# Expert blocks of two halves of 64 slots, side by side in TensorE's column tiles

## The chip, the cores and the metric

The kernel runs on 1 core of one Trainium2 chip. Times are microseconds (us) of device time of one execution; a kernel's time is the median of its runs.

## What is computed

One layer on `x` of shape (2, 1024, 256): a spiking recurrence, a gated mixture of convolutions and a delta-rule attention, a second recurrence, and a mixture of eight experts. Only the last part is touched:

```python
xf = x.reshape(-1, d)                      # 2048 tokens of 256
logits = xf @ gate_w.T + gate_b
top1 = jnp.argmax(logits, axis=-1)         # one expert per token
for e in range(8):
    h = jax.nn.relu(xf @ w1[e].T + b1[e])  # 256 -> 1024
    y = h @ w2[e].T + b2[e]                # 1024 -> 256
    out = out + jnp.where((top1 == e)[:, None], y, 0)
```

Its result is added to the residual stream. Everything is fp32.

## The kernel before

The stages run one after the other, each a function with its own block of per-engine programs: `load_and_spike`, `project`, `fir`, `attend`, `mix`, `recur`, `experts`. They are joined by semaphores written out by hand, and each engine does its instructions in the order of its program. `project` and `fir` matter here only as places where TensorE already works in column tiles: at L372 four matmuls with 32 columns of weights write partitions 0, 32, 64 and 96 of one bank, and at L574 sixteen to thirty-two such matmuls follow each other, four by four. A matmul in fp32 leaves two records in the trace, each with its own load of weights.

`experts` sorts the 2,048 tokens by expert, so that each token is computed by its own expert alone. First the routing: VectorE finds each token's expert (`hot`), TensorE counts them (L1881, L1882), VectorE works out how many blocks of 128 slots each expert needs (`more`, `nblk`, `first`, L1994 to L1999), each token's slot (`place`, `slot`), and from that the lists `slot_token` (which token sits in a slot) and `eid_i` (which expert a block belongs to). An expert's tokens fill whole blocks, the last one in part, so up to 16 + 7 = 23 blocks (`BLOCKS`) are always computed; empty slots hold an index out of range and are skipped by the transfers. Meanwhile TensorE turns the state `h` into rows (`turn`, L1874), ScalarE copies them and writes them to memory (`h_rows`, L1952, L1954), and the weights `w2` of six experts are still being loaded (L1829); `w1`, all of it, and `w2` of two experts are there already.

Then the blocks, g = 0 to 22:

- GpSimd fetches the block's rows of `h` (`fetch_x`, L1843) and of the residual (`fetch_z`, L1851) by indirect transfers into two buffers each, and at the end scatters the result `y` to `out` (L1862). Its order is: fetch x of g+3, wait for y of g, scatter it, fetch z of g+2.
- TensorE: `turn_in` (L1902) turns the rows, two matmuls of 128 columns; `hidden` (L1911) multiplies them by `w1` of the block's expert, 2 halves n x 2 parts c, 512 columns each; `turn_hidden` (L1929) turns the 1,024 hidden values in eight matmuls; `output` (L1920) multiplies by `w2`, 8 parts k, 256 columns each. The order is: `hidden(g)`, `turn_in(g+1)`, `output(g-1)`, `turn_hidden(g)`. The expert's number is read into a register (L1933), and the weights are addressed with it.
- VectorE copies `hid` out of its banks (L2059), copies the turned input (`xt`, L2052), and adds the residual (L2067) and the bias `b2` (L2069) to the result. Its order is: `hid_out(g)`, `x_out(g+1)`, `y_out(g-1)`.
- ScalarE adds `b1` and applies the relu, on the way from the turned bank to `ht` (L1962), eight operations a block.

Of the kernel before, what the change touches and what calls it, by code (L numbers as in the profile page):

```python
# [19 lines left out]
P = 128  # L20
# [18 lines left out]
BLOCKS = B * T // P + E - 1  # L39
# [1429 lines left out]
def expert_constants(sb):  # L1469
# [7 lines left out]
    g.edges = sb("moe_edges", [P, TILES])  # L1477
    g.ids = sb("moe_ids", [P, BLOCKS])
# [283 lines left out]
def experts(nc, d, m, out):  # L1762
# [5 lines left out]

    TOK = B * T
    TILES = TOK // P  # L1770
    K2 = EH // P
    with ExitStack() as own:
# [14 lines left out]
        more = sb("more", [P, E, TILES])  # L1787
# [10 lines left out]
        upto = sb("upto", [P, BLOCKS, E])  # L1798
        eid = sb("eid", [P, BLOCKS])
        eid_i = own.enter_context(nc.sbuf_tensor("eid_i", [1, BLOCKS], I32))  # L1800
        row = free_zw.rearrange("p (a n) -> p a n", n=D)
        xin = [sb(f"xin{i}", [P, D]) for i in range(2)]
# [11 lines left out]
                 "ht_psum", "ht_ready", "y_psum", "y_half", "y_ready")  # L1814
# [5 lines left out]
        out_rows = out.rearrange("b t d -> (b t) d")  # L1820
        block = own.enter_context(nc.Block())
# [47 lines left out]
        def _(pe):  # L1869
# [62 lines left out]
            def expert(g):  # L1932
                return pe.value_load(eid_i[0:1, g:g + 1], min_val=0, max_val=E - 1)  # L1933
# [15 lines left out]
        def _(act):  # L1949
# [6 lines left out]
            for g in range(BLOCKS):  # L1956
                e = act.value_load(eid_i[0:1, g:g + 1], min_val=0, max_val=E - 1)
                if g:
                    act.wait_ge(s.y_psum, g)
                for k in range(K2):  # L1960
                    act.wait_ge(s.ht_psum, g * 2 + (k // (K2 // 2) + 1))
                    nc.scalar.activation(ht[:, k, :], tr_bank[k // (K2 // 2)][:, k % (K2 // 2) * P:(k % (K2 // 2) + 1) * P],  # L1962
                                         ACT.Relu, bias=b1[:, bass.ds(e, 1), k]).then_inc(s.ht_ready, 1)

        @block.vector
        def _(dve):
# [27 lines left out]
            nc.vector.tensor_tensor(more[:], cum[:, :, TILES].unsqueeze(2).broadcast_to([P, E, TILES]),  # L1994
                                    edges[:].unsqueeze(1).broadcast_to([P, E, TILES]), ALU.is_gt).then_inc(s.r, 1)
# [7 lines left out]
            nc.vector.scalar_tensor_tensor(place[:], wide(first), float(P), by_tile, ALU.mult,  # L2003
# [22 lines left out]
            for part in (slice(0, TILES // 2), slice(TILES // 2, TILES)):  # L2026
# [4 lines left out]
            nc.vector.tensor_tensor(upto[:], first[:].unsqueeze(1).broadcast_to([P, BLOCKS, E]),  # L2031
                                    ids[:].unsqueeze(2).broadcast_to([P, BLOCKS, E]), ALU.is_le).then_inc(s.r, 1)
# [14 lines left out]

            def x_out(g):
# [12 lines left out]
            def y_out(g):  # L2061
                e = dve.value_load(eid_i[0:1, g:g + 1], min_val=0, max_val=E - 1)
# [161 lines left out]
```

## Time and profile before

| | |
|---|---|
| median of 3 runs | 989.38 us (986.22 to 990.27) |
| the profiled execution, its own time | 986.34 us |
| its span | 984.4 us |
| busy: TensorE, its weight loads, VectorE, ScalarE, GpSimd | 74%, 46%, 67%, 52%, 26% |
| mean granted clock of TensorE | 0.871 |
| start of the stage `experts`, of its first `hidden`, end of the span | 756.5, 785.9, 984.4 us |

The busy shares are means over stages with different limits; what a change of one stage is worth is read in that stage. A record of TensorE lasts from its start to its modelled end, and consecutive ones overlap, so the distance between two starts is the cost of one, not its length. Where the chain of waits names an instruction, the length is its share of the chain. Instructions are named by line of the kernel before.

### The profile page before, as it was taken

Reading aid. Unit: us, or ns where it says so; the run is one execution under the profiler, and the core shown is the slowest. Engines: PE = TensorE matmul, PEld = TensorE weight load, DVE = VectorE, ACT = ScalarE, POOL = GpSimd, SP = SyncE. Lnnn points to the kernel's source line nnn. Section 1 sums busy time; section 2 is a strip of 40 time slices with the busy share of each in tenths; the row PEclk is TensorE's granted clock in tenths of the full one; section 3 lists DMA queues with packets and bytes.
Section 4 is the critical chain, followed back from the end, with each engine's and each line's share of the span. In section 5 each row is a group of like instructions: output and inputs, shape, how many; then the busy total and the mean of one; then the engine's idle time right before and its main releaser. Section 6 shows DMA issues by size and latency. Waiting matters only on the chain. (4 is left out here: it accounts for less than half of the span.)

```text
span 984.4 us, 15091 instructions
## 1 busy us (share of the span) xinstructions
PE 724.7 (74%) x5694; PEld 451.0 (46%) x5694; DVE 656.4 (67%) x929; ACT 514.6 (52%) x842; POOL 257.6 (26%) x231
## 2 busy tenths in 40 slices
PE   2840009787766187783986878999997599999995
PEld 1310004333555186772443443444446466777763
DVE  4999986967745987357698744999997233333331
ACT  5878764753333353555562348999993122222221
POOL 0000000001102000000332403988994223433331
PEclk9985558988999678997987889999996599999998
DMA  5640000001891000003000017600002811111100
GB/s 200 219 134 0 0 0 22 1 0 43 229 252 35 1 3 24 3 3 99 1 0 1 22 65 267 233 1 1 0 1 60 299 32 39 45 43 37 38 12 0
DMA packets 35881, 60.68 MB, mean 62 GB/s; under 512 B 8187, under 2 KB 22523, under 8 KB 35426
## 3 DMA queue, kind: packets, MB, share of 16 engines
q1 hardware_dynamic: 30194, 51.31, 16.6%
q0 software_dynamic: 3312, 6.31, 2.1%
q10 hardware_dynamic: 2304, 2.10, 0.6%
q8 instruction: 47, 0.77, 0.3%
q14 instruction: 24, 0.20, 0.1%
HBM read 55.23 MB, written 7.21 MB: 63 GB/s over the span
## 5 line engine op out<-in xcount | busy, mean ns | idle before, releaser
L1962 ACT ACTIVATE xT<-x_tr,moe_b 128x128 f32<-128x128 f32 x184 | 50.1, 383 | 145.5 <-PE x_tr L1929 145.5
L1911 PE MATMUL x_hid<-w,moe_xt 128*128 x184 | 84.6, 603 | 0.9 <-DVE moe_xt L2052 0.7
L1920 PE MATMUL x_y<-w,xT 128*128 x368 | 83.3, 379 | 2.1 <-ACT xT L1962 2.1
L1159 POOL TENSOR_TENSOR path<-path,mix_pr 128x1280 f32<-128x1280 f32 x16 | 38.7, 2448 | 144.8 <-DVE mix_pr L1393 144.8
L2059 DVE COPY xT<-x_hid 128x512 f32<-128x512 f32 x46 | 31.9, 692 | 63.5 <-PE x_hid L1911 63.5
L1920 PEld LDWEIGHTS x_y<-w,xT 128*128 128x128 f32 x368 | 68.2, 190 | 11.1 <-issue 2.8
L1713 DVE TENSOR_TENSOR_SCAN w<-r_bank,w 128x512 f32<-128x512 f32 x56 | 69.7, 1246 | 0.2 <-ACT r_bank L1647 0.2
L217 PE MATMUL bad_sum<-spike_bad,ones 128*128 128x16 f32 x2 | 0.6, 384 | 84.1 <-ACT spike_outside L183 84.1
L1587 PE MATMUL r_bank<-recur_h_other,w1h 128*128 128x512 f32 x128 | 60.3, 593 | 0.7 <-ACT recur_h_other L1627 0.7
L1583 PE MATMUL r_bank<-hs,eye 128*128 128x512 f32 x112 | 57.2, 592 | 1.8 <-DVE h L1694 1.8
L213 PE MATMUL w_bank<-spike_wbuf,spike_pick 128*128 128x512 f32 x80 | 39.6, 650 | 23.3 <-DMA spike_wbuf<-in_gW 23.3
L475 DVE SCALAR_TENSOR_TENSOR proj_y<-proj_pre,mix_st,proj_y 128x1024 f32<-128x1024 f32 x36 | 46.2, 1284 | 10.9 <-ACT proj_y L438 9.8
L2067 DVE TENSOR_TENSOR moe_y<-x_y,moe_zin 128x256 f32<-128x256 f32 x23 | 9.7, 423 | 64.1 <-PE x_y L1920 64.1
L1862 POOL DMA_INDIRECT out<-moe_y,slot_token x23 | 23.6, 1026 | 107.4 <-DVE moe_y L2069 107.4
L1911 PEld LDWEIGHTS x_hid<-w,moe_xt 128*128 128x128 f32 x184 | 33.8, 194 | 35.6 <-issue 35.6
L1673 POOL TENSOR_TENSOR w<-w,recur_h_other 128x512 f32<-128x512 f32 x32 | 37.8, 1182 | 45.8 <-ACT w L1637 45.2
L390 PE MATMUL pj<-hs,mix_st 128*128 128x512 f32 x96 | 45.8, 624 | 2.3 <-PEq L65 2.3
L1587 PE MATMUL r_bank<-h,w1h 128*128 128x512 f32 x96 | 45.1, 592 | 0.0
L1701 DVE TENSOR_TENSOR r_bank<-r_bank,xT 128x512 f32<-128x512 f32 x56 | 38.1, 680 | 8.1 <-ACT r_bank L1633 8.1
L1647 ACT ACTIVATE r_bank<-r_bank,recur_leak,recur_leak_neg 128x512 f32<-128x512 f32 x56 | 42.1, 751 | 1.9
L649 DVE COPY path<-fir_z_bank 64x256 f32<-64x256 f32 x64 | 27.0, 422 | 21.6 <-PE fir_z_bank L584 20.0
L161 ACT ACTIVATE spike_count<-spike_line,spike_mid 128x2048 int16<-128x2048 f32 x8 | 39.1, 4887 | 1.1 <-DVE spike_line L244 1.1
(286 smaller groups left out, 1769.2 us busy)
## 6 DMA issues: line engine op xcount, KB each, us to landing
spike_wbuf<-in_gW SPq DMA_DIRECT2D x8, 1280.0 KB, 6.3
w<-in_w1T SPq DMA_DIRECT2D x8, 1024.0 KB, 12.1
w<-in_w2T SPq DMA_DIRECT2D x8, 1024.0 KB, 14.5
fir_band<-in_band_l SPq DMA_DIRECT2D x11, 512.0 KB
fir_band<-in_band_m SPq DMA_DIRECT2D x11, 312.0 KB
mix_st<-in_band_l SPq DMA_DIRECT2D x5, 512.0 KB
xT<-in_xT SPq DMA_DIRECT2D x4, 512.0 KB, 6.7
xT<-in_xT SPq DMA_DIRECT2D x2, 1024.0 KB, 6.1
```

What stands on the lines that cost most here:

```text
L161: nc.scalar.activation(count[i][:, 2:].rearrange("p (t s) -> p s t", s=SUB), line[u % 2][:], ACT.Relu, bias=mid[:]).then_inc(rounded, 1)
L213: last = nc.tensor.matmul(w_bank[:], pick[:, at:at + P], wbuf[:, ch % 2, i, :], start=(ch == 0 and i == 0), stop=(ch == CHUNKS - 1 and i = ...
L390: last = nc.tensor.matmul(pj[u % 2][:, n * N:(n + 1) * N], w[:, i, k, c * P:(c + 1) * P], m.hs[:, k * B + b, n * N:(n + 1) * N], start=(k ...
L475: nc.vector.scalar_tensor_tensor(out, pre[:, u % 2, k:k + T], wc[:, i, c, k:k + 1], out, ALU.mult, ALU.add).then_inc(conv_step if k < KQ - ...
L1159: nc.gpsimd.tensor_tensor(x, x, w, ALU.mult).then_inc(s.weighted, 1)
L1583: nc.tensor.matmul(out, m.eye[:], zw[:, c * B + b, t0:t0 + N], start=True, stop=False)
L1587: last = nc.tensor.matmul(out, wg[:, k, c * P:(c + 1) * P], state[u // UNITS % 2][:, k * B + b, t0:t0 + N], start=False, stop=(k == C - 1))
L1647: nc.scalar.activation(out, out, ACT.Identity, bias=leak[:, c:c + 1], scale=leak_neg[:, c:c + 1]).then_inc(s.j_ready, 1)
L1713: nc.vector.tensor_tensor_scan(change[:, r, :], j_bank[u % RING][:], rest[:, r, :], first, ALU.mult, ALU.add).then_inc(s.change_ready, 1)
L1911: last = nc.tensor.matmul(hid_bank[n][:], xt[:, c, :], m.w1[:, bass.ds(e, 1), c, n * N:(n + 1) * N].rearrange("p o n -> p (o n)"), start=( ...
L1920: last = nc.tensor.matmul(y_bank[:], ht[:, k, :], w2[:, bass.ds(e, 1), k, :].rearrange("p o n -> p (o n)"), start=(k == 0), stop=(k == K2 ...
L1962: nc.scalar.activation(ht[:, k, :], tr_bank[k // (K2 // 2)][:, k % (K2 // 2) * P:(k % (K2 // 2) + 1) * P], ACT.Relu, bias=b1[:, bass.ds(e, ...
```

## The change

A block of 128 slots becomes two halves of 64, and each half has its own expert. The slots of an expert are padded to whole halves, so 32 + 7 halves at most, in (32 + 8) / 2 = 20 blocks. `eid_i` has an entry for each half. Where one matmul took 128 columns of weights (the tokens) and multiplied them by one expert's matrix, there are now two with 64 columns each, into partitions 0 to 63 and 64 to 127 of the same bank (`side(0)`, `side(1)`). The first reads its expert's matrix in place, addressed by a register; the second reads a copy with a fixed address: `w1_copy`, made by GpSimd (`copy_w1`), and `w2_copy`, made by VectorE (`copy_w2`), two buffers each, in room that the states `h` and `hs` leave free. TensorE waits for `w1_copied` before `hidden` and for `w2_copied` before `output`, which now waits for its activations in two parts. ScalarE makes 16 operations of 64 columns for 8 of 128, and VectorE adds `b2` half by half. The turns stay as they were.

```diff
-BLOCKS = B * T // P + E - 1
+HALF = P // 2
+BLOCKS = (B * T // HALF + E) // 2
...
+        w2_copy = free_zw[:, 0:2 * K2 * D].rearrange("p (i k n) -> p i k n", i=2, k=K2)
+        w1_copy = m.h[:].rearrange("p j t -> p (j t)")[:, 0:2 * C * EH].rearrange("p (i c n) -> p i c n", i=2, c=C)
...
+            def copy_w1(g):
+                if g >= BLOCKS:
+                    return
+                if g >= 2:
+                    pool.wait_ge(s.hid_psum, 2 * (g - 1))
+                e = pool.value_load(eid_i[0:1, 2 * g + 1:2 * g + 2], min_val=0, max_val=E - 1)
+                nc.gpsimd.tensor_copy(w1_copy[:, g % 2], m.w1[:, bass.ds(e, 1)].rearrange("p o c n -> p (o c) n")).then_inc(s.w1_copied, 1)
+
+            pool.wait_ge(s.turned, TILES)
+            pool.wait_ge(s.eid_ready, 1)
+            copy_w1(0)
...
             fetch_x(2)
+            copy_w1(1)
             for g in range(BLOCKS):
                 fetch_x(g + 3)
-                pool.wait_ge(s.y_ready, g + 1)
+                copy_w1(g + 2)
+                pool.wait_ge(s.y_ready, 2 * (g + 1))
...
             def hidden(g, e):
                 pe.wait_ge(s.xt_ready, g + 1)
+                pe.wait_ge(s.w1_copied, g + 1)
                 for n in range(EH // N):
+                    cols = slice(n * N, (n + 1) * N)
                     if g:
                         pe.wait_ge(s.hid_ready, 2 * (g - 1) + n + 1)
                     for c in range(C):
-                        last = nc.tensor.matmul(hid_bank[n][:], xt[:, c, :], m.w1[:, bass.ds(e, 1), c, n * N:(n + 1) * N].rearrange("p o n -> p (o n)"),
-                                                start=(c == 0), stop=(c == C - 1))
+                        nc.tensor.matmul(hid_bank[n][side(0), :], xt[:, c, side(0)],
+                                         m.w1[:, bass.ds(e, 1), c, cols].rearrange("p o n -> p (o n)"),
+                                         start=(c == 0), stop=(c == C - 1), skip_group_check=True)
+                        last = nc.tensor.matmul(hid_bank[n][side(1), :], xt[:, c, side(1)], w1_copy[:, g % 2, c, cols],
+                                                start=(c == 0), stop=(c == C - 1), skip_group_check=True)
                     last.then_inc(s.hid_psum, 1)
 
             def output(g, e):
-                pe.wait_ge(s.ht_ready, g * K2 + K2)
+                pe.wait_ge(s.w2_copied, g + 1)
                 if g:
                     pe.wait_ge(s.y_half, g)
                 for k in range(K2):
-                    last = nc.tensor.matmul(y_bank[:], ht[:, k, :],
-                                            w2[:, bass.ds(e, 1), k, :].rearrange("p o n -> p (o n)"), start=(k == 0), stop=(k == K2 - 1))
+                    if k % (K2 // 2) == 0:
+                        pe.wait_ge(s.ht_ready, 2 * (g * K2 + k + K2 // 2))
+                    nc.tensor.matmul(y_bank[side(0), :], ht[:, k, side(0)],
+                                     w2[:, bass.ds(e, 1), k, :].rearrange("p o n -> p (o n)"),
+                                     start=(k == 0), stop=(k == K2 - 1), skip_group_check=True)
+                    last = nc.tensor.matmul(y_bank[side(1), :], ht[:, k, side(1)], w2_copy[:, g % 2, k, :],
+                                            start=(k == 0), stop=(k == K2 - 1), skip_group_check=True)
                 last.then_inc(s.y_psum, 1)
...
                 for k in range(K2):
                     act.wait_ge(s.ht_psum, g * 2 + (k // (K2 // 2) + 1))
-                    nc.scalar.activation(ht[:, k, :], tr_bank[k // (K2 // 2)][:, k % (K2 // 2) * P:(k % (K2 // 2) + 1) * P],
-                                         ACT.Relu, bias=b1[:, bass.ds(e, 1), k]).then_inc(s.ht_ready, 1)
+                    turned = tr_bank[k // (K2 // 2)][:, k % (K2 // 2) * P:(k % (K2 // 2) + 1) * P]
+                    for x in range(2):
+                        nc.scalar.activation(ht[:, k, side(x)], turned[:, side(x)], ACT.Relu,
+                                             bias=b1[:, bass.ds(e[x], 1), k]).then_inc(s.ht_ready, 1)
...
+            def copy_w2(g):
+                if g >= BLOCKS:
+                    return
+                if g >= 2:
+                    dve.wait_ge(s.y_psum, g - 1)
+                e = dve.value_load(eid_i[0:1, 2 * g + 1:2 * g + 2], min_val=0, max_val=E - 1)
+                nc.vector.tensor_copy(w2_copy[:, g % 2], w2[:, bass.ds(e, 1)].rearrange("p o k n -> p (o k) n")).then_inc(s.w2_copied, 1)
...
                 dve.wait_ge(s.y_half, g + 1)
-                nc.vector.tensor_tensor(y[g % 2][:], y[g % 2][:], b2[:, bass.ds(e, 1), :].rearrange("p o n -> p (o n)"),
-                                        ALU.add).then_inc(s.y_ready, 1)
-
+                for x in range(2):
+                    nc.vector.tensor_tensor(y[g % 2][side(x)], y[g % 2][side(x)],
+                                            b2[side(x), bass.ds(e[x], 1), :].rearrange("p o n -> p (o n)"),
+                                            ALU.add).then_inc(s.y_ready, 1)
+
+            dve.wait_ge(s.w2_in, 16 * (E - W2_AHEAD))
+            dve.wait_ge(s.rows_out, 16 * TILES)
+            copy_w2(0)
             x_out(0)
+            copy_w2(1)
             for g in range(BLOCKS):
                 hid_out(g)
                 if g + 1 < BLOCKS:
                     x_out(g + 1)
                 if g:
                     y_out(g - 1)
+                    copy_w2(g + 1)
             y_out(BLOCKS - 1)
```

How the orders stand, on two engines. `ISA` is the reading of an address register, `TENSOR_LOAD` the load of the expert's number. TensorE, one `hidden` of a block, before (`w` is `w1`):

```order
L1911 ISA
L1911 MATMUL x_hid<-w,moe_xt 128x512
L1911 ISA
L1911 MATMUL x_hid<-w,moe_xt 128x512
L1911 ISA
L1911 MATMUL x_hid<-w,moe_xt 128x512
L1911 ISA
L1911 MATMUL x_hid<-w,moe_xt 128x512
L1902 MATMUL x_x<-eye,moe_xin 128x128 x2
```

and in the changed kernel (`h` is the room of the copy of `w1`), its first three pairs:

```order
L1934 ISA
L1934 MATMUL x_hid<-w,moe_xt 64x512
L1937 MATMUL x_hid<-h,moe_xt 64x512
L1934 ISA
L1934 MATMUL x_hid<-w,moe_xt 64x512
L1937 MATMUL x_hid<-h,moe_xt 64x512
L1934 ISA
L1934 MATMUL x_hid<-w,moe_xt 64x512
L1937 MATMUL x_hid<-h,moe_xt 64x512
```

Each matmul has become two of half the height, of which only the first needs a register. GpSimd, one turn of its loop, before:

```order
L1862 DMA out<-moe_y,slot_token 2048x256
L1851 DMA moe_zin<-z_rows,slot_token 128x256
L1843 DMA moe_xin<-h_rows,slot_token 128x256
L1862 DMA out<-moe_y,slot_token 2048x256
```

and in the changed kernel:

```order
L1883 DMA out<-moe_y,slot_token 2048x256
L1870 DMA moe_zin<-z_rows,slot_token 128x256
L1862 DMA moe_xin<-h_rows,slot_token 128x256
L1846 TENSOR_LOAD eid_i
L1846 ISA x2
L1847 ISA
L1847 COPY h<-w 128x2048
L1883 DMA out<-moe_y,slot_token 2048x256
```

A copy of 128 x 2048 elements now stands between the fetch of x and the wait for the next result.

## Rows read from the trace of the kernel before

**Rows 1.** Page: head, and the granted clock in 40 slices, in tenths.
```profile
span 984.4 us, 15091 instructions
...
PEclk9985558988999678997987889999996599999998
```

**Rows 2.** Chain that ended last, experts: start us, us, what (a steady block).
```profile
873.00 3.44 PE x_hid L1911 x8
876.44 0.22 PE x_x L1902 x2
876.66 3.46 PE x_y L1920 x16
880.11 0.87 PE x_tr L1929 x8
```

**Rows 3.** Instructions by line and form: xcount | busy us, mean ns | idle, releaser.
```profile
L1911 PE MATMUL x_hid<-w,moe_xt 128*128 x184 | 84.6, 603 | 0.9 <-DVE moe_xt L2052 0.7 <-issue 0.2
L1920 PE MATMUL x_y<-w,xT 128*128 x368 | 83.3, 379 | 2.1 <-ACT xT L1962 2.1
```

**Rows 4.** Timeline, TensorE, stages with column tiles: start us, us, engine, line.
```profile
169.49 0.16 PEld L372 LDWEIGHTS ps<-proj_sq,mix_st 128*32 128x32 f32 x8
169.49 1.07 PE L372 MATMUL ps<-proj_sq,mix_st 128*32 128x512 f32 x8
170.49 3.70 PE L390 MATMUL pj<-hs,mix_st 128*128 128x512 f32 x8
...
208.28 3.60 PE L390 MATMUL pj<-hs,mix_st 128*128 128x512 f32 x8
211.81 1.07 PE L372 MATMUL ps<-proj_sq,mix_st 128*32 128x512 f32 x8
...
252.20 2.18 PE L574 MATMUL fir_y_bank<-fir_band,fir_vt 128*32 128x128 f32 x64 [0.68 <-ACT fir_vt L611]
254.55 0.66 PE L584 MATMUL fir_z_bank<-eye,w1h 128*128 128x128 f32 x4 [0.17 <-ACT w1h L623]
```

**Rows 5.** Timeline, one steady block, VectorE, ScalarE, GpSimd and the transposes.
```profile
871.97 1.04 PE L1929 MATMUL x_tr<-eye,xT 128*128 128x128 f32 x8
...
872.74 0.43 DVE L2069 TENSOR_TENSOR moe_y<-moe_y,b 128x256 f32<-128x256 f32 x1
872.76 2.18 ACT L1962 ACTIVATE xT<-x_tr,moe_b 128x128 f32<-128x128 f32 x8 [5.81 <-PE x_tr L1929]
873.99 1.03 POOL L1862 DMA_INDIRECT out<-moe_y,slot_token  x1 [4.31 <-DVE moe_y L2069]
...
874.76 0.69 DVE L2059 COPY xT<-x_hid 128x512 f32<-128x512 f32 x1 [1.59 <-PE x_hid L1911]
875.33 1.04 POOL L1851 DMA_INDIRECT moe_zin<-z_rows,slot_token  x1 [0.30 <-issue]
...
876.67 1.00 POOL L1843 DMA_INDIRECT moe_xin<-h_rows,slot_token  x1 [0.31 <-issue]
```

**Rows 6.** Instructions by line and form, whole span: the nearest rows for the copies.
```profile
L549 POOL COPY path<-fir_vt 128x2048 f32<-128x2048 f32 x2 | 4.0, 2024 | 14.3 <-DVE xT L640 14.3
L1673 POOL TENSOR_TENSOR w<-w,recur_h_other 128x512 f32<-128x512 f32 x32 | 37.8, 1182 | 45.8 <-ACT w L1637 45.2
L468 DVE TENSOR_SCALAR proj_y<-proj_pre,mix_st 128x1024 f32<-128x1024 f32 x8 | 5.9, 736 | 8.8 <-ACT proj_pre L434 8.8
L235 DVE TENSOR_SCALAR w1h<-xT 128x512 f32<-128x512 f32 x8 | 3.4, 423 | 4.1 <-DMA xT<-in_xT 4.1
L1424 DVE TENSOR_TENSOR mix_o<-mix_o,mix_rs 128x1024 f32<-128x1024 f32 x3 | 3.7, 1225 | 0.1
```

**Rows 7.** Windows before the first block: us, busy by engine, PEclk, DMA share, GB/s.
```profile
780.00:782.00 2.00, 0.00 (x0) 0.00 (x0) 0.00 (x0) 0.00 (x0) 0.62 (x1) 0.50 0.74 247
782.00:783.00 1.00, 0.00 (x0) 0.00 (x0) 0.00 (x0) 0.00 (x0) 0.69 (x2) 0.50 0.00 1
```

More of the change, by code:

```diff
@@ L1476, in expert_constants @@
     g.before = sb("moe_before", [P, P])
-    g.edges = sb("moe_edges", [P, TILES])
-    g.ids = sb("moe_ids", [P, BLOCKS])
+    g.edges = sb("moe_edges", [P, B * T // HALF])
+    g.ids = sb("moe_ids", [P, 2 * BLOCKS])
     g.starts = sb("moe_starts", [P, BLOCKS + 1])
@@ L1786, in experts @@
         same = sb("same", [P, E, 1 + TILES])
-        more = sb("more", [P, E, TILES])
+        more = free_z[:, TILES * P:TILES * P + E * TOK // HALF].rearrange("p (e n) -> p e n", e=E)
         nblk = sb("nblk", [P, 1 + E])
@@ L1797, in experts @@
         slot_token = own.enter_context(nc.sbuf_tensor("slot_token", [P, BLOCKS], I32))
-        upto = sb("upto", [P, BLOCKS, E])
-        eid = sb("eid", [P, BLOCKS])
-        eid_i = own.enter_context(nc.sbuf_tensor("eid_i", [1, BLOCKS], I32))
+        upto = free_z[:, TILES * P + E * TOK // HALF:][:, 0:2 * BLOCKS * E].rearrange("p (g e) -> p g e", e=E)
+        eid = sb("eid", [P, 2 * BLOCKS])
+        eid_i = own.enter_context(nc.sbuf_tensor("eid_i", [1, 2 * BLOCKS], I32))
         row = free_zw.rearrange("p (a n) -> p a n", n=D)
+        w2_copy = free_zw[:, 0:2 * K2 * D].rearrange("p (i k n) -> p i k n", i=2, k=K2)
+        w1_copy = m.h[:].rearrange("p j t -> p (j t)")[:, 0:2 * C * EH].rearrange("p (i c n) -> p i c n", i=2, c=C)
         xin = [sb(f"xin{i}", [P, D]) for i in range(2)]
@@ L1813, in experts @@
                  "tokens_ready", "eid_ready", "turned", "row_ready", "picked", "x_psum", "xt_ready", "hid_psum", "hid_ready",
-                 "ht_psum", "ht_ready", "y_psum", "y_half", "y_ready")
+                 "ht_psum", "ht_ready", "y_psum", "y_half", "y_ready",
+                 "w1_copied", "w2_copied")
         s = namedtuple("ExpertSemaphores", names)(*(sem(n) for n in names))
@@ L1820, in experts @@
         out_rows = out.rearrange("b t d -> (b t) d")
+        side = lambda x: slice(x * HALF, (x + 1) * HALF)
         block = own.enter_context(nc.Block())
@@ L1956, in _ @@
             for g in range(BLOCKS):
-                e = act.value_load(eid_i[0:1, g:g + 1], min_val=0, max_val=E - 1)
+                e = [act.value_load(eid_i[0:1, 2 * g + x:2 * g + x + 1], min_val=0, max_val=E - 1) for x in range(2)]
                 if g:
@@ L1993, in _ @@
             dve.wait_ge(s.r, n)
-            nc.vector.tensor_tensor(more[:], cum[:, :, TILES].unsqueeze(2).broadcast_to([P, E, TILES]),
-                                    edges[:].unsqueeze(1).broadcast_to([P, E, TILES]), ALU.is_gt).then_inc(s.r, 1)
+            nc.vector.tensor_tensor(more[:], cum[:, :, TILES].unsqueeze(2).broadcast_to([P, E, TOK // HALF]),
+                                    edges[:].unsqueeze(1).broadcast_to([P, E, TOK // HALF]), ALU.is_gt).then_inc(s.r, 1)
             dve.wait_ge(s.r, n + 1)
@@ L2001, in _ @@
             dve.wait_ge(s.r, n)
-            nc.vector.scalar_tensor_tensor(place[:], wide(first), float(P), by_tile, ALU.mult,
+            nc.vector.scalar_tensor_tensor(place[:], wide(first), float(HALF), by_tile, ALU.mult,
                                            ALU.add).then_inc(s.r, 1)
@@ L2029, in _ @@
                                         ALU.is_equal).then_inc(s.slots_ready, 1)
-            nc.vector.tensor_tensor(upto[:], first[:].unsqueeze(1).broadcast_to([P, BLOCKS, E]),
-                                    ids[:].unsqueeze(2).broadcast_to([P, BLOCKS, E]), ALU.is_le).then_inc(s.r, 1)
+            nc.vector.tensor_tensor(upto[:], first[:].unsqueeze(1).broadcast_to([P, 2 * BLOCKS, E]),
+                                    ids[:].unsqueeze(2).broadcast_to([P, 2 * BLOCKS, E]), ALU.is_le).then_inc(s.r, 1)
             dve.wait_ge(s.r, n + 10)
@@ L2061, in y_out @@
             def y_out(g):
-                e = dve.value_load(eid_i[0:1, g:g + 1], min_val=0, max_val=E - 1)
+                e = [dve.value_load(eid_i[0:1, 2 * g + x:2 * g + x + 1], min_val=0, max_val=E - 1) for x in range(2)]
                 dve.wait_ge(s.y_psum, g + 1)
```

6 lines of the change are left out of this document (3 added, 3 removed).

## Prediction

> **What bounds the kernel now.** The change touches the last stage alone, the experts, so I first asked where that stage lies and whether TensorE's clock is whole there. The 40 slices show a granted clock of 9 tenths or more in the seven slices before the last, which are the blocks from 787 to 960 us; it is low in the two slices before them, and 8 in the last [rows 1]. The chain of waits then says what a block consists of: matmuls of TensorE end to end, 3.44 us `hidden`, 0.22 the turn of the next input, 3.46 `output`, 0.87 the turns of `hid`, so 7.98 us from one `hidden` to the next, with no wait between them [rows 2]. The groups by line agree: over all 23 blocks, TensorE idled 0.9 us before `hidden` and 2.1 before `output` [rows 3]. The timeline shows the others: in one block GpSimd has three transfers to issue (1.03, 1.04 and 1.00), VectorE four short operations and ScalarE eight activations in 2.18 us [rows 5]. So TensorE bounds every block, a record of 512 columns costs 3.44/8 = 0.43 us, one of 256 costs 3.46/16 = 0.216, one of 128 costs 0.87/8 = 0.109.
>
> **What is removed.** Blocks go from 23 to 20 (16 + 7 against (32 + 8)/2); the number is fixed by the code. If a block kept its 7.98 us, this is 3 x 7.98 = 23.9 us less. Everything below is what is paid back.
>
> **The matmuls themselves.** Each matmul of `hidden` and `output` becomes two with 64 columns of weights, so 24 records a block become 48. If the two of a pair run at the same time, a block still needs 7.98. The nearest rows are two stages of this kernel with tiles of 32 columns. At L372 eight records of 512 columns, four tiles, take 1.00 us to the start of the next group, not 8 x 0.43 = 3.44; at L574 64 records of 128 columns end after 2.18, so 16 rounds of four take (2.18 - 0.27)/16 = 0.119 each, near 0.109 [rows 4] (0.27 is what a record lasts beyond its place in the stream: 1.04 for eight against 7 x 0.109 [rows 5]). So tiles do run side by side, and the loss is between 0 and 0.01 us a round. A block has 24 rounds: 0 to 0.24 us. I take 0, because the L574 rounds have four loads of weights in 0.109 us, and `output` has two in 0.216.
>
> **Going in and out of column tiles.** The turns stay 128 wide, so each block goes into column tiles twice and comes out twice. One such excursion is priced from the stage at L372 and its neighbours [rows 4]. In: the eight records at 208.28 would release the next at 208.28 + 3.44 = 211.72, and L372 begins at 211.81: 0.09. Inside: 1.00 for two rounds of 0.43: 0.14. Out: the group behind it takes 3.70 where an undisturbed one takes 3.60: 0.10. Together 0.33 us. Low end 0.29: where turns follow, four of them take 0.66 (L584) against 1.04 - 4 x 0.109 = 0.60, so 0.06 in place of 0.10. High end 0.36: the eight loads of 32 columns at L372 are over in 0.16 us, and 64 columns may show some 0.03 more. I take 0.33, since `hidden` and `output` are streams of the same length as those at L390 and L372. There are 39 excursions (20 `hidden`, 20 `output`, of which the last `hidden` runs straight into `output` 18): 39 x 0.33 = 12.9 us. A block costs 7.98 + 0.66 = 8.64.
>
> **The copy of w1, on GpSimd.** 2,048 elements a partition: L549 did that in 2.02 us [rows 6]. It lies after the three transfers of its turn, and `hidden` waits for it. From the start T of the turns (871.97): the second add of y begins at T + 0.77 and ends at T + 1.20; the added half is another 0.43, with a gap 0.5; GpSimd begins 0.82 later (873.99 against 873.17 [rows 5]), so at T + 2.5, its transfers follow at steps of 1.34, and the copy runs from T + 6.5 to T + 8.5. It is for the `hidden` two blocks on, which begins at T + 0.87 + 3.44 + 0.22 + 3.46 + 0.87 + 3 x 0.33 = T + 9.85. So it is hidden, with 1.3 us to spare. The load of the expert's number on GpSimd has no row; 0 to 0.6 us (two of the gaps of 0.30 between its transfers) still fits.
>
> **The copy of w2, on VectorE.** L235 and L468 took 423 ns for 512 and 736 for 1,024 elements, so 2,048 cost 0.74 + 2 x 0.31 = 1.36 us; at the rate of an operation with two inputs, 1.23 for 1,024 (L1424), about 2.3 [rows 6]. It stands behind the adds of y, so T + 1.7 to T + 3.1 (4.0). Queued behind it are the copies of `hid`, the first of which could begin at T + 3.1; 0.9 late costs nothing, because the turns that need it start after T + 8. Cost 0; if it were not covered, 20 x 1.36.
>
> **ScalarE.** Sixteen activations of 64 columns in place of eight of 128: at most 16 x 0.27 = 4.4 us [rows 5], T + 0.8 to T + 5.2. `output` starts at about T + 5.2 and now asks for the first eight only. Cost 0 in a block.
>
> **Ends.** In the last block nothing covers: the second half add 0.5, and `output`'s second half may wait up to 8 x 0.27 - 8 x 0.216 = 0.4 for activations [rows 5]; 0.7 us together. At the start `copy_w2(0)` needs the last weights; the share of the transfer engines falls from 0.74 to 0.00 at 782 us [rows 7], so it ends at about 783.4, before x is there; while it runs, GpSimd prepares the fetch of x. 0 to 1.4, I take 0.3. Routing: 128 elements more in two operations, 48 fewer in four, at 1 ns each ((0.69 - 0.43)/256 [rows 5]): 0.1. `copy_w1(0)` and `copy_w1(1)` run while GpSimd or TensorE waits for rows anyway: 0.
>
> **Sum.** -23.9 + 12.9 + 0.7 + 0.3 + 0.1 = -9.9 us against the profiled execution, which took 986.34 us (span 984.4): 976.4. The median of the runs shown lies 3.0 higher, 989.38, and on it the forecast is **979.4 us**.
>
> **Rivals.**
> (B) GpSimd becomes the bound, *slower*. The place is TensorE's wait for the copied w1 before `hidden`. GpSimd's turn may grow by 1.3 us free of charge; of each us beyond, half falls on every block, since the chain from one y to the fetch, the copy and the y two blocks later spans two blocks. The gain of 9.9 is gone when it has grown by 1.3 + 2 x 9.9/18 = 2.4 us. For it: no row shows this copy beside VectorE's; at the rate of GpSimd's two-input operation (1,182 ns for 512 [rows 6]) the copy takes 4.7, 2.7 more, and if GpSimd also stands still for VectorE's 1.36 it is 4.1 more: a block of 10.0, 1004 us. Against: L549 ran at 1 ns per element. 1004 us, chance 0.08. The Trainium skill ("SBUF — State Buffer", section "SBUF: two separate sides") has VectorE's copy of fp32 lock GpSimd out of preparing transfers; by it only the part from T + 2.5 to T + 3.1 counts, and no run here shows it yet.
> (C) The weight loads come out into the open. Each of 24 rounds would show a load; all eight loads at L372 are over in 0.16 us, so at most that, and I take 0.1: 24 x 0.1 x 20 = 48 us, 1027 us. Against: at L372 the loads of both rounds are recorded within the first 0.16 us, so before the first round has streamed [rows 4]. Chance 0.04. The Trainium skill ("TensorE: Matmul & The Clock Gate", Part 3, "The mechanism") says that a load overlaps running matmuls only if the row groups differ, which column tiles do not; by that rule this case holds. The rows speak against it.
> (D) The pairs do not overlap at all: 20 x 6.90 more, 1117 us; chance 0.02, against L372 and L574 both [rows 4].
> (E) Excursions are dearer, no change. If each way shows the whole tail of a record (0.16: 3.60 less 3.44) and a load of 0.1 to 0.2, an excursion is 0.6, 39 cost 23.4: 990 us. Half way there, 984 to 990. Chance 0.11.
>
> **Chances and range.** The forecast case has 0.75. Its own range is 972 to 985: excursions at 0.29 (-1.6), an execution like the profiled one rather than the median (-3), rounds at +0.24 a block (+4.8), a fetch held back (+1). To hold 8 in 10 it reaches into E: 971 to 989. What a measurement of this kernel tells from no change is about 0.5%, 4.9 us. Faster by more than that: 0.75; within it: 0.11 (E); slower: 0.14 (B, C and D).
>
> **What would show it.** `hidden` to `hidden` at 8.64 us; pairs of records starting within a few hundredths; eight `hidden` rounds still 3.44 apart from their borders; gaps of about 0.1 at each of four borders; TensorE idle before `hidden` near zero with GpSimd's copy ending over 1 us ahead; GpSimd's COPY at 2.0 and VectorE's at 1.4; granted clock 1.00 from 800 us on. It is wrong if TensorE's waits name GpSimd's copy (B), if records of a pair start 0.2 to 0.4 us apart (C, D), or if the borders are 0.2 or more (E).

## The result, and the profile after

The changed kernel takes 975.69 us (median of 4 runs, 973.89 to 978.99), the kernel before beside it 989.83 (986.22 to 990.97): a ratio of 0.9857 with a 95% interval of 0.9833 to 0.988, 14.1 us less. The forecast was 979.4, range 971 to 989, faster at 0.75.

The profiled execution of the changed kernel was its slowest, 978.99 us. Page, head and granted clock (compare [rows 1]):

```profile
span 977.2 us, 16350 instructions
...
PEclk9985558988898758898879879999998579999998
```

Spans differ by 7.2 us only, medians by 14.1. SyncE's rows show why: the stage `experts` begins with the first load of `w2`, and that came at 756.48 before and at 762.74 after, 6.3 us later, behind stages that the change does not touch.

Timeline of SyncE, kernel before, then changed kernel (start us, us, line, x count):

```profile
756.48 15.71 SPq L1826 DMA_DIRECT2D w<-in_w2T  x6
```
```profile
762.74 17.15 SPq L1833 DMA_DIRECT2D w<-in_w2T  x6
```

So I measure the stage from that load to the end of the span: 227.9 us before, 214.5 after, -13.4, close to the medians. In full_width, whose stages ahead are those of the changed kernel, it came at 758.58: the delay belongs to the execution. Over all profiled executions of this study that load came anywhere from 756.5 to 762.7. A steady block, from the chain (against [rows 2]; `L1934` and `L1937` are the two matmuls of `hidden`, `L1948` and `L1951` those of `output`, `L1960` the turns):

```profile
866.99 1.02 PE x_tr L1960 x8
868.01 0.57 PE x_hid L1934
...
871.60 0.37 PE x_x L1923 x2
871.97 0.36 PE x_y L1948
...
875.57 1.02 PE x_tr L1960 x8
876.60 0.57 PE x_hid L1934
```

`hidden` to `hidden` is 8.58 us where it was 7.98. Each part that begins behind a change of width is longer in its first piece: 0.57 for 0.43, 0.37 for 0.22, 0.36 for 0.216, 1.02 for 0.87. That is 0.15 at each of four borders (a border is the place where a matmul 128 columns wide stands next to one of 64), 0.60 a block. The timeline of TensorE at two of them:

```profile
866.61 0.38 PE L1948 MATMUL x_y<-w,xT 128*64 x1
...
866.92 0.86 PEld L1960 LDWEIGHTS x_tr<-eye,xT 128*128 128x128 f32 x8 [0.38 <-issue]
866.92 1.09 PE L1960 MATMUL x_tr<-eye,xT 128*128 128x128 f32 x8
867.95 0.64 PE L1934 MATMUL x_hid<-w,moe_xt 128*64 x1
...
868.42 0.59 PE L1934 MATMUL x_hid<-w,moe_xt 128*64 x1
868.43 0.59 PE L1937 MATMUL x_hid<-h,moe_xt 128*64 128x512 f32 x1
```

The last round of `output` would have been over at 866.61 + 0.216 = 866.83; the turns begin 0.09 later. The eight turns would have ended at 866.92 + 0.87 = 867.79 and take 0.05 longer (1.09 for 1.04), and `hidden` begins at 867.95, 0.1 behind them. The two of a pair start within 0.01 us, and rounds still cost 0.43 and 0.216. The loads of weights show one thing more. In the kernel before, the first loads of the turns were recorded 0.22 us ahead of their first matmul (871.97 [rows 5]), beside the matmuls of `output`:

```profile
871.75 1.01 PEld L1929 LDWEIGHTS x_tr<-eye,xT 128*128 128x128 f32 x8
```

In the changed kernel the turns' first load (866.92) starts only together with their first matmul, and it is the same at the other three borders of the block: no load runs ahead of a border. How much of the 0.15 is this load and how much is something else, no run separates.

Groups by line and form, whole span (against [rows 3]):

```profile
L1934 PE MATMUL x_hid<-w,moe_xt 128*64 x160 | 74.8, 611 | 1.0 <-DVE moe_xt L2093 0.8 <-issue 0.2
L1948 PE MATMUL x_y<-w,xT 128*64 x320 | 73.3, 382 | 1.8 <-ACT xT L1995 1.8
L1847 POOL COPY h<-w 128x2048 f32 x20 | 37.9, 1896 | 18.5 <-issue 18.4
L1883 POOL DMA_INDIRECT out<-moe_y,slot_token x20 | 26.6, 1329 | 65.0 <-DVE moe_y L2111 62.0 <-issue 3.0
L2087 DVE COPY hs<-w 128x2048 f32 x20 | 24.6, 1228 | 10.2 <-DMA w<-in_w2T 8.6 <-issue 0.7
```

TensorE idled 1.0 us ahead of `hidden` and 1.8 ahead of `output` over the whole stage, and neither wait names a copy. The two copies have the lengths that the nearest rows gave (1.90 and 1.23 for 2.02 and 1.36). GpSimd and VectorE in a steady block:

```profile
868.53 1.23 DVE L2087 COPY hs<-w 128x2048 f32 x1
869.31 1.35 POOL L1883 DMA_INDIRECT out<-moe_y,slot_token  x1 [2.33 <-DVE moe_y L2111]
...
873.31 1.90 POOL L1847 COPY h<-w 128x2048 f32 x1
```

The copy of `w1` ends at 875.21; the `hidden` that needs it begins at 876.53, so 1.3 us are to spare, in nearly every block (0.95 in the one behind a scatter of 1.64 us). The scatter takes 1.35 us beside VectorE's copy, where it took 1.03 [rows 5].

The clock was whole from 800 us on. Windows of the changed kernel (us, PE busy (x) PEld busy (x) DVE busy (x) ACT busy (x) POOL busy (x), PEclk, DMA share, GB/s):

```profile
780.00:790.00 10.00, 1.17 (x6) 1.02 (x6) 0.53 (x3) 0.37 (x1) 4.07 (x3) 0.50 0.88 304
...
800.00:960.00 160.00, 160.00 (x1084) 80.63 (x1082) 76.93 (x128) 62.93 (x298) 93.11 (x70) 1.00 0.12 37
```

At the start the chain (start us, us) now runs over the last load of `w2`, VectorE's first copy of it and, behind that on VectorE, the copy of the first x:

```profile
776.40 13.15 DMA w<-in_w2T
...
790.38 1.25 DVE hs L2087
...
792.10 1.11 PE x_hid L1934
```

And the end, timeline before, then chain after:

```profile
967.55 1.04 PE L1929 MATMUL x_tr<-eye,xT 128*128 128x128 f32 x8
970.65 3.72 PE L1920 MATMUL x_y<-w,xT 128*128 x16 [2.07 <-ACT xT L1962]
976.23 0.99 POOL L1862 DMA_INDIRECT out<-moe_y,slot_token  x1 [5.64 <-DVE moe_y L2069]
```
```profile
960.85 0.60 PE x_tr L1960 x4
...
963.63 0.42 PE x_y L1948
...
969.61 1.00 POOL out L1883
```

**The stage, piece by piece (us)**

| | before | after | |
|---|---|---|---|
| first `w2` load to first `hidden` | 29.4 | 29.4 | 0.0 |
| first to second `hidden` | 7.04 | 7.21 | +0.2 |
| second to last `hidden` | 167.7 (21 blocks) | 154.4 (18 blocks) | -13.3 |
| last `hidden` to the end | 23.7 | 23.5 | -0.3 |

### The profile page after: what moved, and what is told of

Its sections match the earlier page's. It is cut to its first block and busy times, and to the rows that moved or that the text cites. A ratio compares the mean times of both kernels' runs of the same rounds, so it can differ in the third digit from the quotient of the medians.

```text
span 977.2 us, 16350 instructions
## 1 busy us (share of the span) xinstructions
PE 714.4 (73%) x6072; PEld 412.9 (42%) x6072; DVE 684.8 (70%) x954; ACT 530.9 (54%) x978; POOL 293.1 (30%) x242
## 5 line engine op out<-in xcount | busy, mean ns | idle before, releaser
L1995 ACT ACTIVATE xT<-x_tr,moe_b 128x64 f32<-128x64 f32 x320 | 67.7, 361 | 116.0 <-PE x_tr L1960 115.9
L1934 PE MATMUL x_hid<-w,moe_xt 128*64 x160 | 74.8, 611 | 1.0 <-DVE moe_xt L2093 0.8
L1937 PE MATMUL x_hid<-h,moe_xt 128*64 128x512 f32 x160 | 74.8, 611 | 0.0
L1948 PE MATMUL x_y<-w,xT 128*64 x320 | 73.3, 382 | 1.8 <-ACT xT L1995 1.8
L1951 PE MATMUL x_y<-hs,xT 128*64 128x256 f32 x320 | 73.3, 382 | 0.0
L1948 PEld LDWEIGHTS x_y<-w,xT 128*64 128x64 f32 x320 | 42.3, 137 | 25.7 <-issue 5.6
L2100 DVE COPY xT<-x_hid 128x512 f32<-128x512 f32 x40 | 27.6, 691 | 28.2 <-PE x_hid L1937 28.2
L1883 POOL DMA_INDIRECT out<-moe_y,slot_token x20 | 26.6, 1329 | 65.0 <-DVE moe_y L2111 62.0
L1847 POOL COPY h<-w 128x2048 f32 x20 | 37.9, 1896 | 18.5 <-issue 18.4
```

The costliest lines, as they stand in the source:

```text
L1934: nc.tensor.matmul(hid_bank[n][side(0), :], xt[:, c, side(0)], m.w1[:, bass.ds(e, 1), c, cols].rearrange("p o n -> p (o n)"), start=(c == ...
L1937: last = nc.tensor.matmul(hid_bank[n][side(1), :], xt[:, c, side(1)], w1_copy[:, g % 2, c, cols], start=(c == 0), stop=(c == C - 1), skip_ ...
L1948: nc.tensor.matmul(y_bank[side(0), :], ht[:, k, side(0)], w2[:, bass.ds(e, 1), k, :].rearrange("p o n -> p (o n)"), start=(k == 0), stop=( ...
L1951: last = nc.tensor.matmul(y_bank[side(1), :], ht[:, k, side(1)], w2_copy[:, g % 2, k, :], start=(k == 0), stop=(k == K2 - 1), skip_group_c ...
L1995: nc.scalar.activation(ht[:, k, side(x)], turned[:, side(x)], ACT.Relu, bias=b1[:, bass.ds(e[x], 1), k]).then_inc(s.ht_ready, 1)
```

## Experiments

"Stage" is always the profiled execution's, first `w2` load to end; "block" is `hidden` to `hidden`. Ratios are to the kernel before, run beside it; the changed kernel stands at 0.9857, 214.5 us and 8.58 us. full_width and no_w2_copy compute other numbers, since half of the slots get the weights of another expert, so they serve to explain and are no kernels to use.

| run | time, median | ratio (95%) | stage | block |
|---|---|---|---|---|
| full_width | 965.97 | 0.9775 (0.9737 to 0.9813) | 203.5 | 7.98 |
| double_w1_copy | 989.78 | 0.9997 (0.9976 to 1.0019) | 227.2 | 9.39 |
| turns_together | 971.47 | 0.9814 (0.9791 to 0.9836) | 211.4 | 8.35 |
| sides_in_turn | 1030.01, one run | | 268.2 | 11.27 |
| together_ahead | 970.73 | 0.9816 (0.9787 to 0.9845) | 209.3 | 8.28 |
| together_ahead_2 | 971.53 | 0.9817 (0.979 to 0.9844) | 209.1 | 8.28 |
| no_w2_copy | 975.69 | 0.9868 (0.9838 to 0.9898) | 214.3 | 8.58 |
| sides_by_four | 996.15, one run | | 236.5 | 9.61 |
| double_ahead | 975.9, one run | | 214.8 | 8.58 |
| rows_first | 970.9 | 0.982 (0.9798 to 0.9843) | 209.4 | 8.28 |
| x_first | 975.43 | 0.9859 (0.9831 to 0.9886) | 213.2 | 8.28 |
| x_first_two | 970.7 | 0.981 (0.9786 to 0.9835) | 205.9 | 8.28 |

**full_width: what the column tiles cost.**
```diff
-nc.tensor.matmul(hid_bank[n][side(0), :], xt[:, c, side(0)], ...
-last = nc.tensor.matmul(hid_bank[n][side(1), :], xt[:, c, side(1)], w1_copy[...], ...
+last = nc.tensor.matmul(hid_bank[n][:], xt[:, c, :], m.w1[:, bass.ds(e, 1), c, cols]...
```
(and the same in `output`). 

> 20 blocks with both copies and all their waits kept, but each matmul of hidden and output is 128 columns wide again, so no column tiles; the second half of a block is computed with the weights of the first half's expert. Theory (a block is dearer only by its four borders between wide and tiled matmuls, 0.60 us): hidden to hidden falls from 8.58 to 7.98 us, the time from 975.7 to about 964 us, ratio to before 0.974. Rival (what a block costs more comes from the copies, the second half's adds or the halves' activations): 8.58 stays, 976 us. Rival B's mechanism is nearer here than in the changed kernel, since the block is 0.60 shorter and GpSimd's turn is not: the copy of w1 ended 0.95 us before the hidden that needs it, so two blocks together would lack 0.25, 8.1 per block, 966 us.

Chain of a steady block:
```profile
867.16 3.44 PE x_hid L1934 x8
...
875.14 3.44 PE x_hid L1934 x8
```
7.98, to the hundredth the block of before, with both copies and all their waits in place; only two blocks of the twenty took 0.1 us more (8.06 and 8.08). The ratio of 0.9775 holds the theory's 0.974 in its interval, and excludes the rival's (976 us, 0.986). So the copies, the second add and the sixteen activations cost a block nothing, and the 0.60 is the column tiles'. Against the kernel before this one has three blocks less: 227.9 - 203.5 = 24.4, forecast 23.9.

**turns_together: is the cost paid per border?**
```diff
-                if g + 1 < BLOCKS:
-                    turn_in(g + 1)
                 output(g - 1, expert(g - 1))
+                if g + 1 < BLOCKS:
+                    turn_in(g + 1)
```


> TensorE turns the next x behind output, straight ahead of the turns of hid, instead of between hidden and output; VectorE adds y to z, then copies x, then adds b2. So a block goes into column tiles once and comes out once, where it did so twice. Theory (0.30 us per way in and out again): hidden to hidden 8.28 us, about 970 us, ratio 0.980. Rival (a border costs nothing where the turn of x stands between, and all the cost is at the turns of hid): 8.58 stays, 976 us. Rival (the copy of x comes too late for hidden, 0.1 to 0.5 per block, as it has 0.87 us of turns to hide in and takes 0.42 behind the add of y): 8.4 to 8.8 us, 972 to 980 us, with the wait ahead of hidden put down to VectorE's copy of x.

Blocks of about 8.28 and 8.41 us take turns, 8.35 on average (two, of 8.75 and 8.49, stand out). The first is the theory's. The late ones were held up by neither rival: GpSimd's copy, which now begins later because VectorE's adds of `b2` come behind its copy of x, was over at 878.11, and `hidden` began at 878.31.
```profile
876.21 1.90 POOL L1847 COPY h<-w 128x2048 f32 x1
```
```profile
878.31 0.64 PE L1934 MATMUL x_hid<-w,moe_xt 128*64 x1
```

**together_ahead: take that copy off the chain.**
```diff
+            copy_w1(2)
             for g in range(BLOCKS):
                 fetch_x(g + 3)
-                copy_w1(g + 2)
+                copy_w1(g + 3)
```
(and the loads of the experts' numbers for `b2` in `y_out`, ahead of its waits) 

> As turns_together, with two more edits: GpSimd copies w1 three blocks ahead rather than two (the buffer is free as soon as the hidden that read it is done), and VectorE loads the numbers of the experts for b2 before it waits for y. turns_together ran at 8.35 us a block; every second hidden began 0.13 late, 0.10 us behind the end of GpSimd's copy of w1 (its INSTR ended at 878.11, TensorE went on at 878.21). Theory (that copy had become the bound): 8.28 us a block throughout, and 0.6 to 1 us less behind the last block, so about 2 us below turns_together: 969.5 us, ratio to before 0.979. Rival (hidden waited for VectorE's copy of x, which ended at 877.83): 8.35 us stays, 971.5 us, ratio 0.981.

8.28 in every block from the second on, and the stage 2.1 us shorter, as forecast; the copy now ends 9.4 us ahead. The medians of the two kernels can't tell 2 us apart (0.9814 and 0.9816). Run once more beside x_first, it gave the same. 

> The same kernel as together_ahead, for a comparison with x_first on one chip: 8.28 us a block, the stage 209.3 us, ratio to before 0.981.

**double_w1_copy and double_ahead: how near was rival B?**
```diff
-                nc.gpsimd.tensor_copy(w1_copy[:, g % 2], ...
+                for x in range(2):
+                    nc.gpsimd.tensor_copy(w1_copy[:, g % 2], ...
+                    pool.wait_ge(s.w1_copied, 2 * g + x + 1)
```
(and `hidden` waits for two copies a block) 

> GpSimd makes each copy of w1 twice, so its turn grows by 1.9 us; nothing else changes. In the changed kernel the copy ended 0.95 us before the hidden that waits for it (875.57 against 876.53). The step in the prediction (beyond the slack, half of each us falls on a block, because the chain from a y over fetches and copy to the y two blocks later spans two blocks): 0.5 x (1.9 - 0.95) = 0.48 per block, hidden to hidden 9.05 us, 984 us, ratio to before 0.995. Rival, the whole of it falls on every block: 9.5 us, 993 us, ratio 1.003. Rival, the copy is hidden whatever its length below GpSimd's idle time of 2.67 us: 8.58 us, 976 us.

(The 0.95 there was read in the one block whose scatter had taken 1.64 us; the others have 1.31.) The block became 9.39, not 9.05, and the gain was gone, 0.9997. GpSimd and VectorE:
```profile
868.91 3.85 POOL L1848 COPY h<-w 128x2048 f32 x2
...
874.38 1.27 POOL L1885 DMA_INDIRECT out<-moe_y,slot_token  x1 [1.61 <-DVE moe_y L2113]
...
878.30 3.85 POOL L1848 COPY h<-w 128x2048 f32 x2
```
```profile
871.26 0.42 DVE L2110 TENSOR_TENSOR moe_y<-x_y,moe_zin 128x256 f32<-128x256 f32 x1 [2.96 <-PE x_y L1953]
871.83 1.65 DVE L2113 TENSOR_TENSOR moe_y<-moe_y,b 64x256 f32<-64x256 f32 x2
```
The adds of `b2` took 1.65 in place of 0.87: the first of them ended only behind GpSimd's copy (868.91 + 3.85 = 872.76). The scatter waits for these adds, so GpSimd waits in effect for itself. From the end of one pair of copies to the end of the next there are 1.61 until the scatter starts, 1.27 of scatter, the two fetches and their gaps, 2.65, and 3.85 of copies, together 9.38 of the 9.39 us, and no instruction of TensorE is in this round. So GpSimd's round set the block. The chain over two blocks that the theory went by would have given 8.58 + (1.95 - 1.1)/2 = 9.0 (of the slack of 1.3, 1.1 counts, since a waiting `hidden` begins 0.2 behind the copy). In GpSimd's round each us of copy falls on a block whole, as the first rival had it: with 1.95 us less the round is 7.44, 1.14 below the block, and 8.58 + 1.95 - 1.14 = 9.39. Between 0 and 1.95 us of growth no run was made, so this slope is an estimate from one point.

> double_w1_copy with one edit: w1 is copied three blocks ahead. In double_w1_copy every hidden waited for the second copy (0.73 us), 9.38 us a block. Theory (the length of the chain from y over scatter, fetches and copies to hidden is what cost, not GpSimd's total work, which is 1.3 + 1.0 + 1.0 + 3.8 us and gaps in a turn): hidden to hidden 8.58 us, copies ending more than 5 us before the hidden that needs them, about 976 us. Rival (VectorE's first add of b2 stands still while GpSimd copies, 1.20 us in double_w1_copy in place of 0.43, and that is what stretches a block): a block of 8.8 us or more, 980 us or more.

8.58 and 975.9 us, with the copies 4.0 us ahead and not over 5. With the copies further ahead TensorE no longer waited, so the order of waits was what cost. But GpSimd had nothing left: from 816.88 to 852.99 its turns took 9.03 us each, longer than a block, and ate into the lead; from 861.69 on they took 8.58, with no wait for another engine in them. VectorE's add and its copy stood still for longer there, and it cost TensorE nothing:
```profile
864.53 3.15 DVE L2114 TENSOR_TENSOR moe_y<-moe_y,b 64x256 f32<-64x256 f32 x2
865.49 3.94 POOL L1848 COPY h<-w 128x2048 f32 x2
867.71 2.81 DVE L2090 COPY hs<-w 128x2048 f32 x1
```

**no_w2_copy: VectorE's copy.** `copy_w2` is left out, and `output` waits for the loads of `w2` instead. 

> VectorE's copy of w2 is left out; the second half of every block reads the w2 of expert 0 in its place, so it is computed with other numbers. Theory (the copy of 1.23 us lies beside other work and only holds GpSimd up): 8.58 us a block and 975 to 976 us, ratio 0.985, while GpSimd's scatter of y takes 1.03 us in every block, where it took 1.35 beside the copy. Rival (the copies cost blocks time): below 8.5 us a block, under 973 us.

```profile
L1883 POOL DMA_INDIRECT out<-moe_y,slot_token x17 | 17.5, 1030 | 55.6 <-DVE moe_y L2108 52.3 <-issue 3.3
```
8.58 and 214.3 us stay, and the scatter takes 1.03 us. The copy costs GpSimd 0.3 us a turn and a block nothing.

**sides_in_turn and sides_by_four: what makes pairs overlap.**
```diff
-                for k in range(K2):
-                    nc.tensor.matmul(y_bank[side(0), :], ...
-                    last = nc.tensor.matmul(y_bank[side(1), :], ...
+                for k in range(K2):
+                    nc.tensor.matmul(y_bank[side(0), :], ...
+                for k in range(K2):
+                    last = nc.tensor.matmul(y_bank[side(1), :], ...
```
(This is `output` in sides_in_turn; `hidden` likewise.) 

> The same matmuls in another order: in hidden, for each half of the columns, both matmuls of the first 64 slots and then both of the second 64; in output all eight of the first 64 slots and then all eight of the second. Theory (matmuls are started in program order, and one waits for its own column tile only, so that two run side by side only where neighbours in the order lie in different tiles): hidden 10 rounds of 0.43 where there were 8, output 30 of 0.216 where there were 16, so 3.9 us more a block, 12.5 us, 1054 us. Rival (each tile has its own deep queue, and the order does not matter): 8.58 us, 976 us. Rival (matmuls of one side after the other never overlap): 15.5 us, 1112 us.

No theory gave 11.27. The timeline of `output` there:
```profile
879.52 3.02 PE L1949 MATMUL x_y<-w,xT 128*64 x13
882.16 0.43 PE L1953 MATMUL x_y<-hs,xT 128*64 128x256 f32 x1
882.38 0.38 PE L1949 MATMUL x_y<-w,xT 128*64 x1
```
The second tile's first record starts with the first tile's 13th of 16 (882.16), that is, as soon as no more than four records ahead of it in the program are left. `output` so had 12 + 16 = 28 rounds, 12 x 0.216 = 2.6 more. In `hidden`, with four records of one side and then four of the other, all pairs ran side by side, 0.02 to 0.06 us apart, and 8.58 + 2.6 = 11.2.

> In output, four matmuls (8 records) of the first 64 slots, then four of the second, then again four and four; hidden is in pairs as in the changed kernel. Theory from sides_in_turn, where the first record of the second tile began with the 13th of 16 of the first (a matmul starts beside another tile's once at most 4 records of that tile are ahead of it in the program and not done): second tile's first record with the 5th, its ninth with the 17th, so 20 rounds of 0.216 where there were 16: 8.58 + 0.86 = 9.44 us a block. Rival (neighbours only, 2 records): 22 to 24 rounds, 9.9 to 10.3. Rival (the lookahead of sides_in_turn was the end of output being drained, and in the middle the order does not matter): 8.58.

```profile
875.11 1.29 PE L1949 MATMUL x_y<-w,xT 128*64 x5
876.03 0.43 PE L1953 MATMUL x_y<-hs,xT 128*64 128x256 f32 x1
...
876.95 0.43 PE L1949 MATMUL x_y<-w,xT 128*64 x1
```
The second tile starts with the fifth record and the first tile's ninth with the second's fifth: 20 rounds, 0.86. Each of the three switches costs 0.05 more, which makes 9.61 less 8.58. The rule gave the number of rounds; the 0.15 of the switches was not in it (9.44 forecast, 9.61 measured).

**rows_first, x_first, x_first_two: the start of the stage.** The copies made one more stage wait possible: VectorE's `copy_w2(0)` stood ahead of the first x.
```diff
             for e in range(W2_AHEAD, E):
+                if e == (W2_AHEAD + E) // 2:
+                    sp.wait_ge(s.rows_out, 16 * TILES)
```
(and the new order on VectorE) 

> together_ahead with the start of the stage in another order: SyncE loads the last three w2 only when all rows of h_rows are written, and VectorE copies the first x before it waits for w2 (copy_w2(0) and copy_w2(1) come behind the second x). In the changed kernel the last rows were issued at 781.33, landed at 787.1 behind the w2 loads, x was there at 790.6 and the first hidden began 29.4 us behind the first w2 load. Theory (rows that no longer share the transfer engines land in about 2 us, and no copy of w2 stands ahead of the first x): first hidden 3 to 4.5 us earlier, from 29.4 (together_ahead: 30.2) to about 26, the stage from 209.3 to about 206 us, the time 966 us, ratio to before 0.977. Rival (the three late loads of w2 arrive after output(0) asks for them): first hidden earlier, but output(0) waits, no gain.

The rows did land early, GpSimd issued the first fetch at 779.64, but it took 7.12 us:
```profile
779.64 7.12 DMA moe_xin<-h_rows,slot_token
```
It shared the transfer engines with the loads just released: first `hidden` at +30.1 us behind the first load of `w2`, nothing gained.

x_first waits for `x_in[0]` instead. 

> rows_first with one edit: the last three loads of w2 are issued when the first x has been fetched, not when the rows are written. In rows_first the first fetch of x, issued at 779.64, landed at 786.8, 7.1 us later and behind the 3 MB just released, where it took 3.0 us in the kernel before; the first hidden began 30.1 us behind the first load of w2, as without the edit. Theory (the wait for the transfer engines had only moved from the rows to the fetch): the fetch lands in 3 us, first hidden at about 26 us, the three loads land by 35 and VectorE's copy by 36, ahead of output(0) at 37, so the stage takes 205.3 us and the time is about 4 us below together_ahead's. Rival (w2 comes too late for output(0)): first hidden at 26, but an idle time of TensorE of 1 us or more ahead of the first output, put down to VectorE's copy of w2; gain 0 to 3 us.

```profile
780.40 3.05 DMA moe_xin<-h_rows,slot_token
...
784.51 11.74 DMA w<-in_w2T
...
797.15 1.11 PE x_hid L1937
```
The fetch took 3.05 and the first `hidden` came at +26.3. But TensorE's program waits for all of `w2` ahead of the second `hidden`, which needs none of it. I had put that wait at the first `output`; the second `hidden` came at +38.5 instead of +36.6, and the stage took 213.2. The wait is only half of the 4 us lost. Behind it the granted clock, 0.99 from 790 to 795 us, was 0.50 from 795 to 800; the first rounds of `hidden` took 0.84 where they take 0.43, and this block 10.52 us instead of 8.28.

x_first_two moves that wait to the first `output` and holds back two loads. 

> x_first with two edits: only the last two loads of w2 wait for the first x (not three), and TensorE waits for w2 ahead of the first output, not ahead of the second hidden. In x_first the first hidden came 26.3 us behind the first load, but the second waited for w2, which landed at 796.25, and began at 797.15; the clock fell to 0.50 on the way, and the stage took 213.2 us. Theory (the early x is worth what it promised once w2 is waited for where it is needed): first hidden at 26.3 us, second at 33, output(0) at about 37 with w2 landed at 32 and copied at 34, so the stage takes 205.8 us where together_ahead's took 209.2, ratio to before 0.978. Rival (the transfer engines are the bound of the whole start, so what x gains w2 loses): a wait of 1 us or more ahead of output(0), stage 208 us or more.

First `hidden` at +26.7, second at +33.4, no wait ahead of `output`, stage 205.9: the theory's numbers. It is the shortest stage of the kernels that compute the result, yet the median of 970.7 does not show the 3.3 us: its runs lie from 965.2 (the profiled one) to 973.6. In the other kernels with more than one run the median less the stage is 760 to 762.6; here it is 764.8. Whether something ahead of the stage became slower in the runs without a profile, or five runs fell high, stays open.

## Why the prediction was right, step by step

- **What bounds, three blocks less (-23.9).** Right. The stage of full_width is 24.4 shorter than that of before. (VectorE has five operations a block, not four; nothing hung on it.)
- **Matmuls side by side (0).** Right: pairs 0.01 apart, rounds of 0.43 and 0.216. So is the reason given, that loads do not show in a round.
- **Excursions, 0.33 each, 39 of them (+12.9).** The mechanism was right, the size 10% high: 0.30 each, twice shown, by 8.58 to 8.28 with one excursion less and to 7.98 with two less. Over the 36 in the steady blocks that is 1.1 us too much. The term had put 0.14 inside an excursion beside the two borders; measured are two borders of 0.15.
- **Copies of w1 and w2, ScalarE (0).** Right in a block, with the slack of 1.3 us as forecast.
- **Ends, start, routing (+1.1), and three excursions there (+1.0).** Wrong in sign, if small: the piece table gives 0.0 + 0.2 - 0.3. The last `output` began 2.8 us behind the turns where it was 3.1, since it waits for half the activations; I had counted that as a loss. And 0.6 of the tail is the last scatter, 7.6 us from its issue to the end and not 8.2; it is 7.5 to 7.6 in every profile of a kernel with halves, and why stays open. At the start one reading was wrong: `copy_w2(0)` was to end before x is there (783.4, 26.9 us behind the first load of `w2`), but it ended at 791.63, 28.9 behind, and x was there at 790.6. TensorE's turn of x ran beside it, and going by the 0.77 us from that turn to VectorE's copy of x in the kernel before (784.53 to 785.30), the copy of x came about 0.2 late (791.68 for 790.67 + 0.77), near the 0.3 taken.
- **The sum** was -9.9 against the profiled execution; the stage lost 13.4. The difference of 3.5 is 1.1 + 2.2, the two items above, and rounding. The 3.0 added for the median was right to add: what lies ahead of the stage moved by more than that from one execution to another.
- **Rival B** did not come about: no wait of TensorE names the copy. But its price was too low. The prediction let half of each us beyond the slack fall on a block and saw the gain gone at 2.4 us of growth; double_w1_copy grew GpSimd's work by 1.95 and came out at 0.9997, because VectorE's adds sat out the copy and closed a round of GpSimd alone, in which the whole of it falls on a block.
- **Rivals C and D.** Excluded. The Trainium skill ("TensorE: Matmul & The Clock Gate", Part 3, "The mechanism") lets a load overlap only where row groups differ; but the same section also lets a load into the background weight buffer go ahead of running matmuls, which the prediction passed over. Here two tiles share all rows and the loads, 0.14 us each, never showed in a round, so the measurement decides against the first of the two sentences and is in keeping with the second; whether that buffer is the reason, no run shows. The kernel before spoke against it too: its loads for `output`, 128 wide and 0.19 us each, did not show in rounds of 0.216.
- **Rival E** (0.6 per excursion) is excluded by 0.30. That there is a cost agrees with the Trainium skill ("TensorEngine Tiling (Array Packing)", "Key Properties"), by which a change of tiling mode drains the array; the runs put 0.15 us on each change. That the array drains is not shown; that no load runs ahead of a border is.

## What to carry over

A stage bounded by one engine is worth counting in units of that engine: how many blocks, what each costs, and what each border between modes costs, here 0.15 us. A border is paid per change of width, so put the wide work together: moving one pair of turns beside the others gave back 0.30 of the 0.60 us a block. When an engine off the critical path gets more work, look for a round that closes on that engine, not only for the chain to the engine that bounds. And before a load is held back for the sake of another, find every place where the program waits for it, not only the one that needs it.

## What the runs showed of the hardware, not expected

- Matmuls in different column tiles started beside each other although up to four records of the other tile stood ahead in the program, and not beyond: in sides_in_turn the first record of the second tile started with the first tile's 13th of 16, ahead of its 14th to 16th, and in sides_by_four with the 5th of 8.
- At a change between 128 and 64 columns no load of weights ran ahead: the first load started with its matmul (866.92), where in a stream of one width it had started 0.22 us ahead (871.75 for 871.97).
- An addition of two SBUF operands by VectorE waited for a GpSimd copy that was under way: 1.65 for 0.87 in double_w1_copy, while the add that reads PSUM kept its 0.42. In double_ahead the two adds took 3.15; there the second one is recorded from 864.98, 0.5 ahead of the start of GpSimd's first copy, and still ended behind it, at 867.68. The other way round, VectorE's fp32 copy stretched GpSimd's scatter from 1.03 to 1.35. The first and the last agree with the lock that the Trainium skill describes ("SBUF — State Buffer", "SBUF: two separate sides"), by which whichever starts first holds the other up; the case of double_ahead does not follow from it as recorded.
- The stages ahead, untouched by the change, took up to 6.3 us more in one profiled execution than in another, nearly half of the whole gain. Within the stage two executions of one kernel (together_ahead) differed by 0.3 us.
